# A graph-network kernel: the table that steers TensorE in its building stage packed eight steps to a word, and VectorE's key comparisons made for two steps at once

## The chip, the cores and the metric

The kernel runs as one program on one core of a Trainium2 chip. The metric is the time on the device, in microseconds, of one execution; less is better. A profiled execution gives a span (first to last instruction) and the rows quoted here. TensorE's clock has two levels, 1.2 and 2.4 GHz; a row gives the granted clock of a stretch as a share of the higher one.

## What is computed

Four graph layers on 6250 nodes of 64 features and 206250 edges, sorted by destination, each with one of four types:

```python
h = relu(layernorm(x));  x = x + attention(h, edges)          # softmax over a node's edges
h = relu(layernorm(x));  x = x + graph_conv(h, src, dst)      # degree-normalised sum
h = relu(layernorm(x));  x = x + message_mlp(h, edge_attr, src, dst)
h = relu(layernorm(x));  x = x + gru_4_steps(h, src, dst, edge_type)
# a step of the last one:
transformed = einsum('nd,khd->knh', feat, W) + b[:, None, :]
a = segment_sum(transformed[edge_type, src], dst)
feat = gru_cell(a, feat)
```

Three of the four layers need sums over a node's edges. The kernel gets them as dense products with an adjacency table: for a pair of neighbouring destination nodes, a block of 128 rows by 392 columns that counts, for each source node (128 places within a block of sources) and each combination of block of sources, type and which of the two destinations (392), the edges there are.

## The kernel before, in words

The stages are: tables from the edge list (to 329 us of the span), **building** of the adjacency table (329 to 3154 us), attention and graph convolution, the edge MLP, and the four steps of the last layer. The change touches the building stage and the tables made for it.

Edges come in tiles of 128. A pair of destinations may lie across tiles, so the work is a list of `BSTEPS` = 4859 steps; a step adds one tile's edges to one pair's block. There are 3248 pairs (`VW`), so two blocks out of about three steps are finished.

- **VectorE** (`hots_of`, L1802 to L1808) makes for each step two arrays of zeros and ones in a ring of 16 slots, `hots`: three comparisons (TENSOR_SCALAR) of a row of numbers in 16 bits with one 32-bit key a partition: L1805 over 128 columns with `key_lo`, L1806 over 98 with `key_u`, L1807 over 294 with `key_hi`. It waits on `step_done` for a free slot.
- **TensorE** (`count`, L1117 to L1131) runs two matmuls a step: L1127 multiplies the two parts of the slot (128 x 128 by 128 x 392) and adds into one of the 8 banks of `ps`; L1130 is a one-column product of zeros that marks the next bank as fresh and raises `step_done`. Which bank stands in a table, `steptab`, worked out on the chip: a word a step holds both column offsets (`>> 12` and `% 4096`). A second row of it holds, for each group of 4 steps (`BATCH`), the count of evictions that must have happened.
- The loop is written out for 64 steps (`SWEEP`) and runs 75.9 sweeps. `words` (L1109 to L1115) loads 16 words of the table into registers of TensorE's sequencer with one TENSOR_LOAD (all at L1112): once a sweep the 16 waits, which stand four words apart, and at steps 0, 16, 32 and 48 the words of 16 steps, which stand side by side. That is five loads a sweep.
- Before each group of 4 the sequencer waits for `hot_made` (L1125, L1126) and `evicted`. Before each matmul it does register arithmetic that turns the word into an address; the profile calls it FUSED_REGOPS.
- **ScalarE** (`evict`, L831 to L844) copies each finished block from its bank to `stagebuf`, with a table of its own (L835). **SyncE** (`keep`, from L616) stores 16 finished blocks at a time to HBM, 203 such events of two transfers each. **GpSimd** (`mark`) tells ScalarE when a part of `stagebuf` is free.

```python
nc.tensor.matmul(ps[:, bass.ds(held["banks"][j % STEPW] >> 12, 2 * COMBS)], hots[:, j % BRING, 0:P], ...)      # L1127
nc.tensor.matmul(ps[:, bass.ds(held["banks"][j % STEPW] % 4096, 1)], zero16[:, :], zero16[:, 0:1], ...)          # L1130
nc.vector.tensor_scalar(hots[:, j, 0:P], count_lo[:, :], part(key_lo[:, :], k, 1), None, ALU.is_equal)           # L1805
```

Ahead of the stage VectorE works out the table's columns (L1685 to L1694), TensorE turns them, L1700 copies them to `tabi`, and SyncE sends them through HBM into `steptab`. Right before the first step L1796 to L1800 derive `key_u` from `key_hi`: one copy, and three times a TENSOR_SCALAR and a TENSOR_TENSOR over 4864 columns in 32 bits. VectorE, TensorE, ScalarE, SyncE and GpSimd each run a program of their own in the order written; semaphores alone tie them.

Of the kernel before, what the change touches and what calls it, by code (L numbers as in the profile page):

```python
# [7 lines left out]
P = 128  # L8
# [3 lines left out]
NB = -(-N // P)  # L12
# [68 lines left out]
STEPW, VIRTW, BATCH = 16, 16, 4  # L81
ENDBITS = 13
SWEEP = 64
PRE = 8
# [69 lines left out]
def build(nc, a, out):  # L154
    ctx = ExitStack()
    with ctx:
# [16 lines left out]
        step_rows = dram("step_rows", (3 * BC, P), I32)  # L173
# [9 lines left out]
        key_u = early[:, 0:BPAD]  # L183
# [56 lines left out]
        tabcols = here("tabcols", [P, 3 * BC])  # L240
        tabi = here("tabi", [P, P], I32)
# [316 lines left out]
        def _(sp):  # L558
# [41 lines left out]
            def table(n, rows, count, into, first=0):  # L600
# [3 lines left out]
                sp.wait_ge(tab_stored, 16 * (n + 1))  # L604
# [4 lines left out]
            table(0, step_rows, 3, steptab)  # L609
# [4 lines left out]
            sp.wait_ge(tab_loaded, 16 * 10)  # L614
# [16 lines left out]
            sp.wait_ge(hot_made, BSTEPS)  # L631
# [85 lines left out]
        def _(pool):  # L717
# [58 lines left out]
            pool.wait_ge(tab_loaded, 16 * 10)  # L776
# [243 lines left out]
        def _(pe):  # L1020
# [53 lines left out]
            turn_table(0, 3 * BC)  # L1074
# [31 lines left out]
            pe.wait_ge(tab_loaded, 16 * 10)  # L1106
# [1152 lines left out]
```

## Time and profile before

| | |
|---|---|
| median of 3 runs | 14162.31 us (14157.45 to 14164.72) |
| the profiled execution's own time | 14159.53 us |
| its span | 14157.8 us |
| building stage, first TensorE instruction of the loop to the last matmul | 329.8 to 3153.4 us |
| busy in the whole span | TensorE 10878.2 us (77%), VectorE 6203.7 (44%), ScalarE 3496.2 (25%), GpSimd 4392.1 (31%) |
| granted clock, whole span | 0.895 |

An instruction's duration in a row runs from its start to its end; instructions of one engine overlap, so what one costs in a stream is the distance between starts. Rows of a sequencer carry a q (PEldq, DVEq, ACTq): loads of registers, register arithmetic, branches. A sequencer handles them one after the other, and an engine's instruction isn't sent before those ahead of it are done. "Idle before it" names what ended last before an instruction by the profile's own inference.

### The profile page before, as it was taken

What the parts mean: (1) busy time and instruction counts of PE and PEld (TensorE: products, weight loads), DVE (VectorE), ACT (ScalarE), POOL (GpSimd) and SP (SyncE); (2) the same over time, 40 slices, a digit from 0 to 9 for tenths busy, and PEclk for the clock granted to TensorE, in tenths of its full rate; (3) what the DMA queues carried; (4) which work ended last, traced back from release to release, by engine and by line L of the source; (5) the groups of instructions that cost most, each with busy time, mean ns of one, the idle gap of its engine ahead of it and who ended that gap; (6) DMA issues with size and microseconds to landing.
All of it is one profiled execution on the core that took longest, in us unless ns stands there. A gap on an engine that the chain in (4) does not pass through costs nothing.

```text
span 14157.8 us, 274727 instructions
## 1 busy us (share of the span) xinstructions
PE 10878.2 (77%) x60251; PEld 6423.2 (45%) x60252; DVE 6203.7 (44%) x28648; ACT 3496.2 (25%) x9549; POOL 4392.1 (31%) x3429
## 2 busy tenths in 40 slices
PE   2666656559997677777777777777789999999999
PEld 2333333333334555555555555555644444444443
DVE  6999999885662433333333343334221111111111
ACT  0555545553330222222222222222100000000000
POOL 2000000000000688888888888888200000000000
PEclk8676676769998899999999999999689999999999
DMA  2333333332226233333333333333579899899898
GB/s 93 114 115 115 115 113 114 111 128 87 94 89 264 37 42 42 42 42 42 42 42 42 42 42 42 42 42 42 46 288 348 330 355 350 336 353 348 336 348 308
DMA packets 1120461, 2096.68 MB, mean 148 GB/s; under 512 B 372941, under 2 KB 982880, under 8 KB 1012496
## 3 DMA queue, kind: packets, MB, share of 16 engines
q1 hardware_dynamic: 823736, 1913.57, 37.9%
q0 software_dynamic: 295904, 174.34, 12.0%
q8 instruction: 249, 4.08, 0.1%
q14 instruction: 572, 4.69, 0.1%
HBM read 1630.27 MB, written 457.23 MB: 147 GB/s over the span
## 4 chain that ended last, share of the span: by engine, by line
PE 51%; issue 20%; POOL 13%; DVE 9%; DMA 2%; ACT 1%; DVEq 1%; SPq 1%; POOLq 1%; ACTq 0%; another core or an unknown queue 0%
PE ps L1479 16%; PE ps L1484 8%; PE ps L1127 8%; POOL G L491 7%; POOL reverse L811 7%; PE ps L1182 4%; DVE hots L1807 2%; DVE hots L1805 2%; PE ps L1173 2%; DMA reverse<-SD,sidx 2%; DVE hots L1806 2%; PE ps L1331 1%; PE ps L1342 1%; PE ps L1282 1%; PE ps L1332 1%
## 5 line engine op out<-in xcount | busy, mean ns | idle before, releaser
L811 POOL DMA_INDIRECT reverse<-SD,sidx x1660 | 2649.2, 1596 | 555.5 <-issue 496.8
L1127 PE MATMUL ps<-hots 128*128 128x392 f16 x4859 | 1709.1, 440 | 1111.3 <-DVE hots L1807 564.9
L1479 PE MATMUL ps<-chunk,feat 128*128 128x512 f16 (+1 forms) x10192 | 2278.6, 375 | 15.0 <-DVE feat L2169 14.0
L491 POOL DMA_INDIRECT G<-h_table,idx x1660 | 1649.8, 994 | 1942.8 <-issue 1929.7
L2006 DVE TENSOR_TENSOR acc<-acc,ps 128x132 f32 x1660 | 485.5, 292 | 3014.4 <-PE ps L1345 2960.2
L841 ACT ACTIVATE stagebuf<-ps 128x392 f32 x3248 | 1438.2, 508 | 1416.1 <-PE ps L1130 1351.6
L1342 PE MATMUL ps<-MS,OH 128*128 128x128 f32 x3320 | 773.9, 316 | 1194.0 <-issue 798.1
L1479 PEld LDWEIGHTS ps<-chunk,feat 128*128 128x128 bf16 x10192 | 943.4, 98 | 1301.2 <-issue 308.0
L1807 DVE TENSOR_SCALAR hots<-count_hi,key_hi 128x294 f16<-128x294 f16 x4859 | 1458.6, 300 | 0.0
L918 ACT ACTIVATE SD<-ps 128x129 f32<-128x129 f32 x1660 | 462.0, 278 | 3701.8 <-DMA reverse<-SD,sidx 3692.0
L1805 DVE TENSOR_SCALAR hots<-count_lo,key_lo 128x128 f16<-128x128 f16 x4859 | 1240.3, 255 | 258.6 <-PE ps L1130 258.1
L1342 PEld LDWEIGHTS ps<-MS,OH 128*128 128x128 f32 x3320 | 545.0, 198 | 1741.4 <-issue 1717.9
L1127 PEld LDWEIGHTS ps<-hots 128*128 128x128 f16 x4859 | 593.8, 122 | 1622.2 <-issue 1351.3
L1331 PE MATMUL ps<-early,OT 128*128 128x256 f32 x3320 | 1081.3, 409 | 251.4 <-issue 225.2
L2105 DVE TENSOR_TENSOR summed<-ps,upper 64x512 f32<-64x512 f32 (+1 forms) x208 | 139.5, 671 | 2580.9 <-ACT upper L971 2580.8
L1806 DVE TENSOR_SCALAR hots<-count_hi,early 128x98 f16<-128x98 f16 x4859 | 1235.8, 254 | 0.0
L1484 PE MATMUL ps<-chunk,feat 128*64 128x512 f16 (+1 forms) x10192 | 1212.5, 377 | 0.0
L1332 PE MATMUL ps<-big,OT 128*128 x3320 | 1047.3, 399 | 0.0
L1130 PE MATMUL ps<-zero 128*128 128x1 bf16 x4859 | 950.8, 196 | 0.0
L798 POOL DMA_INDIRECT slot_rows<-first_table,slot_of x2 | 1.9, 956 | 2914.2 <-DMA first_table<-H 2913.9
L1345 PE MATMUL ps<-MS,EQ 128*128 128x129 f32 x3320 | 813.4, 328 | 0.0
L1484 PEld LDWEIGHTS ps<-chunk,feat 128*64 128x64 bf16 x10192 | 515.0, 109 | 655.8 <-issue 301.3
(417 smaller groups left out, 14411.3 us busy)
## 6 DMA issues: line engine op xcount, KB each, us to landing
chunk<-adj SPq DMA_DIRECT2D x720, 1792.0 KB, 9.0
adj<-stagebuf SPq DMA_DIRECT2D x406, 784.0 KB, 5.6
chunkA<-adj SPq DMA_DIRECT2D x48, 1792.0 KB, 6.7
chunk<-adj SPq DMA_DIRECT2D x60, 1232.0 KB, 6.8
G<-in_edge SPq DMA_DIRECT2D x1660, 32.0 KB
G<-h_table,idx POOLq DMA_INDIRECT x1660
reverse<-SD,sidx POOLq DMA_INDIRECT x1660
reverse<-acc SPq DMA_DIRECT2D x4, 3225.0 KB, 20.0
```

Of the source, the lines that this page charges most:

```text
L491: nc.gpsimd.indirect_dma_start(G[:, j, 0:width], None, table, bass.IndirectOffsetOnAxis(idx[:, j:j + 1], 0))\
L811: nc.gpsimd.indirect_dma_start(reverse[j % R], bass.IndirectOffsetOnAxis(sidx[:, j:j + 1], 0), SD[:, j % R, :], None, compute_op=ALU.add). ...
L841: nc.scalar.activation(stagebuf[:, bass.ds(held["word"][j] >> ENDBITS, SLEN)].rearrange("p (x c) -> p x c", c=BLK)[:, :, 0:2], bank[j % 8] ...
L1127: nc.tensor.matmul(ps[:, bass.ds(held["banks"][j % STEPW] >> 12, 2 * COMBS)], hots[:, j % BRING, 0:P], hots[:, j % BRING, P:P + 2 * COMBS] ...
L1331: nc.tensor.matmul(bank[2 + j % 2][:, 0:2 * M], OT[:, j % 2, 0:P], w("edge"), start=True, stop=False)
L1332: nc.tensor.matmul(bank[2 + j % 2][:, 0:2 * M], OT[:, j % 2, P:2 * P], big[:, bass.ds(b * 2 * M, 2 * M)], start=False, stop=True).then_inc ...
L1342: nc.tensor.matmul(bank[6][:, 0:M], OH[:, j % HOT, :], MS[:, j % MR, 0:M], start=True, stop=True)
L1479: nc.tensor.matmul(bank[k % 2][:, 0:cols], feat[0][:, hi, 0:2, :].rearrange("p a d -> p (a d)"), columns(chunk4, i % DRING, m, cols), star ...
L1484: last = nc.tensor.matmul(bank[k % 2][half:half + D, 0:cols], feat[0][:, hi, 2, :], columns(chunk4, i % DRING, m, cols), start=False, stop ...
L1805: nc.vector.tensor_scalar(hots[:, j, 0:P], count_lo[:, :], part(key_lo[:, :], k, 1), None, ALU.is_equal)
L1806: nc.vector.tensor_scalar(hots[:, j, P:P + 2 * NB], count_hi[:, 0:2 * NB], part(key_u, k, 1), None, ALU.is_equal)
L1807: nc.vector.tensor_scalar(hots[:, j, P + 2 * NB:P + 2 * COMBS], count_hi[:, 2 * NB:2 * COMBS], part(key_hi[:, :], k, 1), None, ALU.is_equa ...
```

## The change

Three things change in the building stage.

1. **TensorE's table.** A step's bank is kept as 3 bits, eight steps to a word; two group waits of 12 bits share a word. So 8 words of banks and 8 of waits serve 64 steps, and they stand side by side in one row: one load of 16 words a sweep in place of five of 16. Addresses are now worked out as `word >> 3 * i`, `% 8 * 512` for L1139 (before L1127) and `+ 1, % 8 * 512` for L1142 (before L1130), with multiply and add for size and base in both as before. Every second group takes one shift more for its wait.
2. **VectorE's comparisons.** `hots` is a ring of 8 slots for two steps each, the two interleaved: element i of step 0, element i of step 1. A slot is made by three TENSOR_TENSOR instructions of 16-bit operands: the row of numbers (each twice) against the two keys of the pair, read again for every column. Keys are kept in 16 bits. TensorE reads its operands from `hots` at every second element.
3. **The tables' making.** The packing is done by VectorE in 12 small instructions where L1700 was one copy; five small ones ahead of it go. Two transfers and one load replace one and three on SyncE's queue. `key_u` is derived in 16 bits.

```diff
-STEPW, VIRTW, BATCH = 16, 16, 4
+HG = 2
+HGROUPS = -(-BSTEPS // HG)
+HRING = BRING // HG
+VIRTW, BATCH = 16, 4
+PACK = 8
...
+SWEEPW = 2 * SWEEP // PACK
+SWEEPS = P // SWEEP
+BROW = 64
...
-        key_u = early[:, 0:BPAD]
+        key_u = early[:, 0:BPAD // 2].bitcast(F16)
...
-        key_lo = here("key_lo", [P, BPAD])
-        key_hi = here("key_hi", [P, BPAD])
-        steptab = here("steptab", [P, BPAD], I32)
+        key_lo = here("key_lo", [P, BPAD], F16)
+        key_hi = here("key_hi", [P, BPAD], F16)
+        steptab = here("steptab", [1, BC * SWEEPS * SWEEPW], I32)
...
-        count_lo = here("count_lo", [P, P], F16)
-        count_hi = here("count_hi", [P, 2 * COMBS], F16)
+        count_lo = here("count_lo", [P, P, HG], F16)
+        count_hi = here("count_hi", [P, 2 * COMBS, HG], F16)
...
-        hots = here("hots", [P, BRING, P + 2 * COMBS], F16)
+        hots = here("hots", [P, HRING, P + 2 * COMBS, HG], F16)
...
-        hots_f = stagebuf[:, 0:2 * BPAD].bitcast(F32)
+        hots_f = stagebuf[:, 0:BPAD]
...
-            table(0, step_rows, 3, steptab)
+            sp.wait_ge(tab_copied, 1)
+            for kind, row in enumerate((BROW, 0)):
+                sp.dma_start(step_rows[:, :, kind, :], tabi[row:row + BC, 0:P // PACK].rearrange("c (s w) -> c s w", s=SWEEPS))\
+                    .then_inc(tab_stored, 16)
+            sp.wait_ge(tab_stored, 32)
+            sp.dma_start(steptab[0:1, :], step_rows.rearrange("(o c) s k w -> o (c s k w)", o=1)).then_inc(tab_loaded, 16)
...
-            def words(row, k, n, stride, top):
+            def words(it):
                 _, v = nc.values_load_multi_w_load_instructions(
-                    steptab[row:row + 1, k:k + (n - 1) * stride + 1:stride] if known(k) else
-                    steptab[row:row + 1, bass.ds(k, n, step=stride)], engines=(pe.engine,),
-                    min_val=0 if row else 1, max_val=top,
+                    steptab[0:1, it * SWEEPW:(it + 1) * SWEEPW] if known(it) else steptab[0:1, bass.ds(it * SWEEPW, SWEEPW)],
+                    engines=(pe.engine,), min_val=0, max_val=max(8 ** PACK - 1, (VW + 8) * 4097),
                     skip_runtime_bounds_check_because="the path's tables are made of counts within these bounds")
                 return v
 
             def count(k, j, it):
                 if j == 0:
-                    held["free"] = words(0, k + BATCH - 1, SWEEP // BATCH, BATCH, VW + 8)
-                if j % STEPW == 0:
-                    held["banks"] = words(32, k, STEPW, 1, 7 * 512 * 4097)
+                    held["words"] = words(it)
                 if j % BATCH == 0:
-                    pe.wait_ge(hot_made, min(k + BATCH, BSTEPS) if known(k) else k + BATCH)
-                    pe.wait_ge(evicted, held["free"][j // BATCH] & 4095)
-                nc.tensor.matmul(ps[:, bass.ds(held["banks"][j % STEPW] >> 12, 2 * COMBS)], hots[:, j % BRING, 0:P],
-                                 hots[:, j % BRING, P:P + 2 * COMBS],
+                    free, odd = held["words"][SWEEPW // 2 + j // PACK], j // BATCH % 2
+                    pe.wait_ge(hot_made, min((k + BATCH) // HG, HGROUPS) if known(k) else it * (SWEEP // HG) + (j + BATCH) // HG)
+                    pe.wait_ge(evicted, (free >> 12) & 4095 if odd else free & 4095)
+                window = held["words"][j // PACK] >> 3 * (j % PACK)
+                nc.tensor.matmul(ps[:, bass.ds(window % 8 * 512, 2 * COMBS)], hots[:, j // HG % HRING, 0:P, j % HG],
+                                 hots[:, j // HG % HRING, P:P + 2 * COMBS, j % HG],
                                  start=False, stop=True, skip_group_check=True)
-                nc.tensor.matmul(ps[:, bass.ds(held["banks"][j % STEPW] % 4096, 1)], zero16[:, :], zero16[:, 0:1],
+                nc.tensor.matmul(ps[:, bass.ds((window + 1) % 8 * 512, 1)], zero16[:, :], zero16[:, 0:1],
                                  start=True, stop=True, skip_group_check=True).then_inc(step_done, 1)
...
-            link(scalar_(i1, i0, 7, 9, ALU.bitwise_and, ALU.arith_shift_left))
-            link(copy_(f7, i1))
-            link(scalar_(f0, step_w, 1.0, None, ALU.add))
-            link(copy_(i0, f0))
-            link(scalar_(i1, i0, 7, 9, ALU.bitwise_and, ALU.arith_shift_left))
-            link(nc.vector.memset(tabcols[:, 2 * BC:3 * BC], 0.0))
-            link(copy_(tabcols[:, BC:2 * BC], i1))
-            both_(out=tabcols[:, BC:2 * BC], in0=f7, scalar=4096.0, in1=tabcols[:, BC:2 * BC], op0=ALU.mult,
-                  op1=ALU.add).then_inc(tab_cols, 1)
+            link(scalar_(i1, i0, 7, None, ALU.bitwise_and))
+            copy_(tabcols[:, BROW:BROW + BC], i1).then_inc(tab_cols, 1)
...
-            copy_(tabi[0:3 * BC, :], bank[7][0:3 * BC, 0:P]).then_inc(tab_copied, 1)
+            turned_free, turned_bank = (bank[7][row:row + BC, 0:P].rearrange("c (w i) -> c w i", i=PACK) for row in (0, BROW))
+            pack_free, pack_bank = packed[0:BC, :], packed[BROW:BROW + BC, :]
+            link(copy_(pack_free, turned_free[:, :, BATCH - 1]))
+            link(both_(out=pack_free, in0=turned_free[:, :, PACK - 1], scalar=4096.0, in1=pack_free, op0=ALU.mult, op1=ALU.add))
+            link(copy_(pack_bank, turned_bank[:, :, 0]))
+            for i in range(1, PACK):
+                link(both_(out=pack_bank, in0=turned_bank[:, :, i], scalar=float(8 ** i), in1=pack_bank, op0=ALU.mult, op1=ALU.add))
+            link(copy_(tabi[0:BC, 0:P // PACK], pack_free))
+            copy_(tabi[BROW:BROW + BC, 0:P // PACK], pack_bank).then_inc(tab_copied, 1)
...
+            def keys_of(keys, k, columns):
+                return part(keys[:, :], k, HG).unsqueeze(1).to_broadcast([P, columns, HG])
+
             def hots_of(k, j, it):
-                if not (known(k) and k < BRING):
-                    v.wait_ge(step_done, k - BRING + 1)
-                nc.vector.tensor_scalar(hots[:, j, 0:P], count_lo[:, :], part(key_lo[:, :], k, 1), None, ALU.is_equal)
-                nc.vector.tensor_scalar(hots[:, j, P:P + 2 * NB], count_hi[:, 0:2 * NB], part(key_u, k, 1), None, ALU.is_equal)
-                nc.vector.tensor_scalar(hots[:, j, P + 2 * NB:P + 2 * COMBS], count_hi[:, 2 * NB:2 * COMBS],
-                                        part(key_hi[:, :], k, 1), None, ALU.is_equal).then_inc(hot_made, 1)
-            pipeline(v, BSTEPS, BRING, 0, lambda it, j: stage(BSTEPS, BRING, it, j, 0, hots_of))
+                if not (known(k) and k < HRING):
+                    v.wait_ge(step_done, k * HG - BRING + HG)
+                nc.vector.tensor_tensor(hots[:, j, 0:P, :], count_lo[:, :, :], keys_of(key_lo, k, P), ALU.is_equal)
+                nc.vector.tensor_tensor(hots[:, j, P:P + 2 * NB, :], count_hi[:, 0:2 * NB, :], keys_of(key_u, k, 2 * NB), ALU.is_equal)
+                nc.vector.tensor_tensor(hots[:, j, P + 2 * NB:P + 2 * COMBS, :], count_hi[:, 2 * NB:2 * COMBS, :],
+                                        keys_of(key_hi, k, 2 * COMBS - 2 * NB), ALU.is_equal).then_inc(hot_made, 1)
+            pipeline(v, HGROUPS, HRING, 0, lambda it, j: stage(HGROUPS, HRING, it, j, 0, hots_of))
```

TensorE, at the head of a sweep, before. ISA is the register arithmetic ahead of a matmul, REGISTER_ALU a single register operation:

```order
563 L134 UNCONDITIONAL_BRANCH
564 L134 ISA
565 L1112 TENSOR_LOAD steptab
566 L1112 ISA
567 L1112 TENSOR_LOAD steptab
568 L1125 REGISTER_ALU
569 L1126 REGISTER_ALU [waits hot_made]
570 L1127 ISA [waits evicted]
571 L1127 MATMUL ps<-hots 128x392
572 L1130 ISA
573 L1130 MATMUL ps<-zero 128x1
```

The same place after the change, and the head of the second group of 4:

```order
570 L1125 TENSOR_LOAD steptab
571 L1136 ISA
572 L1137 REGISTER_ALU [waits hot_made]
573 L1139 ISA [waits evicted]
574 L1139 MATMUL ps<-hots 128x392
...
589 L1136 REGISTER_ALU
590 L1137 REGISTER_ALU [waits hot_made]
591 L1137 REGISTER_ALU
592 L1139 ISA [waits evicted]
593 L1139 MATMUL ps<-hots 128x392
```

One load stands where two stood (three more go later in the sweep), and each step keeps two ISA and two MATMUL; what an ISA holds grew from three register operations to five (at a word's first step four for L1139).

VectorE in the loop, one step before:

```order
285 L1804 REGISTER_ALU
286 L1805 ISA [waits step_done]
287 L1805 TENSOR_SCALAR hots<-count_lo,key_lo 128x128
288 L1806 REGISTER_ALU
289 L1806 TENSOR_SCALAR hots<-count_hi,early 128x98
290 L1807 REGISTER_ALU
291 L1807 TENSOR_SCALAR hots<-count_hi,key_hi 128x294
```

and two steps after the change:

```order
261 L1821 ISA
262 L1822 ISA [waits step_done]
263 L1822 TENSOR_TENSOR hots<-count_lo,key_lo 128x256
264 L1823 REGISTER_ALU
265 L1823 TENSOR_TENSOR hots<-count_hi,early 128x196
266 L1824 REGISTER_ALU
267 L1824 TENSOR_TENSOR hots<-count_hi,key_hi 128x588
```

Three instructions now make two steps, twice as wide each; `early` is the memory that holds `key_u`.

## Rows read from the trace of the kernel before

**Rows 1.** Busy time by stretch, 600 us inside the building stage.
```profile
core 0: us, PE busy (x) PEld busy (x) DVE busy (x) ACT busy (x) POOL busy (x), PEclk, DMA share, GB/s
1000.00:1600.00 600.00, 365.01 (x2072) 220.52 (x2072) 543.98 (x3098) 303.49 (x684) 0.00 (x0) 0.70 0.34 113
```
**Rows 2.** Waits, 329 to 3160 us: who waited for whom, us in total, times, longest.
```profile
PEld ps L1127 <- issue: 1351.3, 1217, 9.4
PE ps L1127 <- DVE hots L1807: 564.9, 277, 5.8
DVE hots L1805 <- PE ps L1130: 258.1, 100, 5.7
```
**Rows 3.** TensorE's timeline: start us, duration us, instruction; firsts of groups of 4, and two steps.
```profile
1500.51 0.49 PE L1127 MATMUL ps<-hots 128*128 128x392 f16 x1
1500.86 0.49 PE L1127 MATMUL ps<-hots 128*128 128x392 f16 x1
...
1506.93 0.34 PE L1127 MATMUL ps<-hots 128*128 128x392 f16 x1 [1.44 <-DVE hots L1807]
...
1508.39 0.49 PE L1127 MATMUL ps<-hots 128*128 128x392 f16 x1 [0.16 <-issue]
```
**Rows 4.** Line L1112, whole trace; then two stretches of one sweep (min/median/max ns).
```profile
L1112 PEldq TENSOR_LOAD <-steptab x380: 1102/1274/7260, 329.9 to 3147.1; - x190
...
L1112 PEldq TENSOR_LOAD <-steptab x3: 1103/2002/5232, 1104.9 to 1117.4; - x3
...
L1112 PEldq TENSOR_LOAD <-steptab x2: 1107/1862/2617, 1125.5 to 1132.6; - x2
```
**Rows 5.** TensorE's timeline on both sides of a single load and of a sweep's head.
```profile
1097.06 0.34 PE L1127 MATMUL ps<-hots 128*128 128x392 f16 x1
1098.86 0.51 PE L1127 MATMUL ps<-hots 128*128 128x392 f16 x1 [1.46 <-DVE hots L1807]
...
1104.21 0.34 PE L1127 MATMUL ps<-hots 128*128 128x392 f16 x1
...
1111.80 0.50 PE L1127 MATMUL ps<-hots 128*128 128x392 f16 x1 [7.25 <-issue]
```
**Rows 6.** Register work of TensorE's sequencer by line: count, min/median/max ns.
```profile
L1127 PEldq FUSED_REGOPS  x4859: 72/76/84, 335.2 to 3153.1; - x195
L1130 PEldq FUSED_REGOPS  x4859: 73/78/89, 335.4 to 3153.3; - x195
L1112 PEldq FUSED_REGOPS  x296: 52/52/58, 368.3 to 3108.0; - x148
L1332 PEldq FUSED_REGOPS  x1660: 55/55/77, 4703.1 to 9989.1; - x185
L134 PEldq FUSED_REGOPS  x131: 44/68/78, 364.2 to 10249.0; - x131
```
**Rows 7.** VectorE's timeline, the same instruction five steps apart.
```profile
1500.44 0.25 DVE L1805 TENSOR_SCALAR hots<-count_lo,key_lo 128x128 f16<-128x128 f16 x1 [0.95 <-PE ps L1130]
...
1503.07 0.25 DVE L1805 TENSOR_SCALAR hots<-count_lo,key_lo 128x128 f16<-128x128 f16 x1
```
**Rows 8.** VectorE's groups by shape: count, busy us, mean ns.
```profile
L1643 DVE TENSOR_SCALAR cmps<-iota,cf 128x4864 bf16<-128x4864 int16 x13 | 18.3, 1482 | 1.0 <-PE ps L1041 1.0
L1800 DVE TENSOR_TENSOR early<-early,stagebuf 128x4864 f32<-128x4864 f32 x3 | 15.7, 5225 | 0.1
L1799 DVE TENSOR_SCALAR stagebuf<-early 128x4864 f32<-128x4864 f32 x3 | 8.1, 2694 | 0.1
```
**Rows 9.** VectorE's timeline: starts of two-source instructions; one small one of the tables.
```profile
5604.82 0.69 DVE L526 TENSOR_TENSOR OH<-iota,dloc 128x512 f32<-128x512 f32 x1
5605.43 0.17 DVE L1994 TENSOR_TENSOR TH<-iota,typ 128x16 f32<-128x16 f32 x1
5605.51 0.35 DVE L2022 TENSOR_SCALAR EQ<-ps,key 128x128 f32<-128x128 f32 x1
...
210.19 0.22 DVE L1689 TENSOR_SCALAR cf<-cf 128x38 f32<-128x38 f32 x1
```
**Rows 10.** ScalarE in the stage: two evictions in the timeline, its table's loads by line.
```profile
1501.50 0.94 ACT L841 ACTIVATE stagebuf<-ps 128x392 f32 x2 [0.20 <-PE ps L1130]
...
L835 ACTq TENSOR_LOAD <-path x203: 1012/1022/1222, 302.2 to 3146.1; - x102
```

More of the change, by code:

```diff
@@ L172, in build @@
         key_table = dram("key_table", (TP, 3 * P))
-        step_rows = dram("step_rows", (3 * BC, P), I32)
+        step_rows = dram("step_rows", (BC, SWEEPS, 2, SWEEPW // 2), I32)
         virt_rows = dram("virt_rows", (3 * VC, P), I32)
@@ L240, in build @@
         tabcols = here("tabcols", [P, 3 * BC])
+        packed = here("packed", [P, P // PACK])
         tabi = here("tabi", [P, P], I32)
@@ L603, in table @@
                 sp.dma_start(rows, tabi[0:rows.shape[0], :]).then_inc(tab_stored, 16)
-                sp.wait_ge(tab_stored, 16 * (n + 1))
+                sp.wait_ge(tab_stored, 16 * (n + 2))
                 lines = rows.rearrange("(q c) p -> q (c p)", q=count)
@@ L613, in _ @@
             sp.dma_start(endrow, virt_rows.rearrange("(q c) p -> q (c p)", q=3)[0:1, :]).then_inc(tab_loaded, 16)
-            sp.wait_ge(tab_loaded, 16 * 10)
+            sp.wait_ge(tab_loaded, 16 * 8)
             def keep(k, j, it):
@@ L630, in _ @@
             pipeline(sp, NEV, 6, 0, lambda it, j: stage(NEV, 6, it, j, 0, keep))
-            sp.wait_ge(hot_made, BSTEPS)
+            sp.wait_ge(hot_made, HGROUPS)
             sp.dma_start(X_, a["x"].rearrange("(b p) d -> p b d", p=P)).then_inc(x_loaded, 16)
@@ L774, in _ @@
                         .then_inc(key_gathered[h], 16)
-            pool.wait_ge(tab_loaded, 16 * 10)
+            pool.wait_ge(tab_loaded, 16 * 8)
             def words(row, k, top):
@@ L1073, in _ @@
                 last.then_inc(cmp_used, 1)
-            turn_table(0, 3 * BC)
+            turn_table(0, BROW + BC)
             pe.wait_ge(asked, 2)
@@ L1103, in _ @@
                 last.then_inc(key_turned, 1)
-            pe.wait_ge(tab_loaded, 16 * 10)
+            pe.wait_ge(tab_loaded, 16 * 8)
             pe.wait_ge(key_copied, 10)
@@ L1625, in _ @@
             link(copy_(at[:, :], at_i[:, :]))
-            link(copy_(count_lo[:, :], iota16[:, 1:P + 1]))
-            link(copy_(count_hi[:, :], iota16[:, 0:2 * COMBS]))
+            link(copy_(count_lo[:, :, :], iota16[:, 1:P + 1].unsqueeze(2).to_broadcast([P, P, HG])))
+            link(copy_(count_hi[:, :, :], iota16[:, 0:2 * COMBS].unsqueeze(2).to_broadcast([P, 2 * COMBS, HG])))
             link(nc.vector.memset(weigh[:, :, :], 1.0))
@@ L1684, in _ @@
             copy_(tidx[:, :], f0).then_inc(step_known, 1)
+            link(nc.vector.memset(tabcols[:, :], 0.0))
             link(scalar_(tabcols[:, 0:BC], step_w, 2.0, None, ALU.add))
             link(copy_(i0, step_w))
-            link(scalar_(i1, i0, 7, 9, ALU.bitwise_and, ALU.arith_shift_left))
-            link(copy_(f7, i1))
-            link(scalar_(f0, step_w, 1.0, None, ALU.add))
-            link(copy_(i0, f0))
-            link(scalar_(i1, i0, 7, 9, ALU.bitwise_and, ALU.arith_shift_left))
-            link(nc.vector.memset(tabcols[:, 2 * BC:3 * BC], 0.0))
-            link(copy_(tabcols[:, BC:2 * BC], i1))
-            both_(out=tabcols[:, BC:2 * BC], in0=f7, scalar=4096.0, in1=tabcols[:, BC:2 * BC], op0=ALU.mult,
-                  op1=ALU.add).then_inc(tab_cols, 1)
+            link(scalar_(i1, i0, 7, None, ALU.bitwise_and))
+            copy_(tabcols[:, BROW:BROW + BC], i1).then_inc(tab_cols, 1)
             for c in range(CG):
@@ L1745, in _ @@
             v.wait_ge(tab_turned, 2)
-            v.wait_ge(tab_stored, 16)
+            v.wait_ge(tab_stored, 32)
             copy_(tabi[0:3 * VC, :], bank[7][0:3 * VC, 0:P]).then_inc(tab_copied, 1)
@@ L1777, in _ @@
             v.wait_ge(tab_turned, 3)
-            v.wait_ge(tab_stored, 32)
+            v.wait_ge(tab_stored, 48)
             copy_(tabi[0:6, :], bank[7][0:6, 0:P]).then_inc(tab_copied, 1)
@@ L1786, in _ @@
                       op0=ALU.is_equal, op1=ALU.mult).then_inc(key_masked, 1)
-            v.wait_ge(tab_loaded, 16 * 10)
+            v.wait_ge(tab_loaded, 16 * 8)
             place = virttab[96:97, 0:VPAD - 1]
```

## The prediction

> **What bounds the kernel now.** I read the busy time of a stretch inside the building stage first [rows 1]: VectorE 544 of 600 us, TensorE 365, granted clock 0.70, DMA share 0.34. That looks like a stage paced by VectorE. The waits say otherwise [rows 2]: VectorE waits 258 us for TensorE's `step_done`, and the largest idle time by far, 1351 us, stands before TensorE's weight load with "issue" as its cause, which is time in which nothing but its own sequencer held it.
>
> So I price the sequencer. Without a load between them, groups of 4 steps start 1.46 us apart (1506.93 to 1508.39), although those four matmuls ran at the high clock (0.34 us each). At the low clock (0.49 us) one step follows another after 0.35 [rows 3], four of them 1.42 us, which the 1.46 also covers. The pace is thus the sequencer's at either clock. A sweep of 64 steps has 16 groups: 23.4 us. The loads come on top [rows 4]: the five of one sweep took 5.23 us at its head, then 1.10, 2.00, 1.11 and 2.62, in sum 12.06. Each costs a restart too: around the load of 1.10 us at 1097 the matmuls of neighbouring groups start 1.80 us apart, around the sweep's head 7.59 [rows 5], where a step across groups without a load takes about 0.5. That is 0.2 us beyond the load for a single one, and 0.75 beyond the two (6.34) at the head. Sum: 23.4 + 12.1 + 0.75 + 3 x 0.2 = 36.8 us. The stage lasts 3153.3 - 329.9 = 2823 us [rows 4, 6] for 75.9 sweeps, 37.2 us each. TensorE's sequencer accounts for the whole stage. VectorE needs 2.63 us for five steps [rows 7], 33.6 us a sweep, and sits in the shadow with 3.6 us to spare, 275 us in all, against 258 measured. The 565 us that the waits give to L1807 can't be a real wait of that size, since the groups leave no room for it; VectorE's signal merely comes last before a matmul that the loads had delayed.
>
> **The change, part by part.**
>
> *Loads.* Four of five go. The remaining one reads 16 words side by side. What does it cost? The cheapest was 1.10 us; the three of the sweep that stood alone took 2.00, 1.11 and 2.62, mean 1.91 [rows 4]. The sweep's first, 5.23 us, has two things apart from them: its words are four apart, and it stands at the loop's head. ScalarE's load of 16 neighbouring words stands at the head of its loop as well and takes 1.01 to 1.22 us [rows 10], so I put the difference down to the spread words and take 2.0. Bounds: 1.1 and 5.2.  With it one restart and the branch, 0.55. Loads and restarts fall from 13.4 (13.8 in the average sweep) to 2.55 us.
>
> The Trainium skill, "Runtime: NRT & Kernel Launch", section on instruction fetch, gives a TENSOR_LOAD about 200 ns a register, however many it loads. An estimate by that page is 3.2 us for the 16 words and a time of 13686. This trace has 69 ns a word where 16 neighbours took 1.10 us, and more than the page where they lie four apart (5.23 us, 327 ns), so I keep the row.
>
> *Register work.* It grows, and it is on the path. Before a matmul three operations (shift or remainder, multiply, add) take 76 and 78 ns [rows 6]. Plain multiplies and adds take 52 for three (L1112), 55 for four (L1332), and 68 where most are the five of a loop's head (L134). So a division costs 24 more than a plain operation, a remainder 26. The new ones: divide, remainder, two multiplies, add: 68 + 24 + 26 = 118, in one step of eight without the division, about 84; mean 114. Add, remainder, two multiplies, add: 68 + 26 = 94. Together 208 where 154 stood, 54 ns a step; I take 56, since the numbers divided are longer. A group: 1.46 + 4 x 0.056 + half a REGISTER_ALU (0.02) = 1.70 us, a sweep 27.2. Bounds: with 5 ns for an added plain operation and 26 for the remainder it is 40 ns a step, group 1.63; with twice the price for division and remainder some 80 to 90, group 1.82.
>
> *TensorE in sum:* 27.2 + 2.55, 29.8 us a sweep, and 0.1 because the stores fill more of each sweep: 29.9. Saved: (37.2 - 29.9) x 75.9 = 554 us.
>
> *VectorE.* No row has a two-source instruction with all operands in 16 bits. From above: in 32 bits an element costs (5225 - 160) / 4864 = 1.04 ns [rows 8]. From below: 16-bit one-source, 1482 ns for 4864 columns, 0.26 with some 0.2 us fixed. I take 0.52, because for one source the step from 32 bits (2694 ns, 0.52) to 16 bits halves an element's price, and the two-source row is the nearer one to start from. The fixed part: an instruction of 16 columns is followed after 0.08 us, one of 512 after 0.61 [rows 9], so about 0.065. A pair of steps: (256 + 196 + 588) x 0.52 + 3 x 0.065 = 0.74 us, a sweep 23.5 us in place of 33.6: still in TensorE's shadow, now by 6.4 us. Only if TensorE's sequencer were cheaper than that would this gain show.
>
> The Trainium skill, "VectorE: DVE Perf Modes", section on the TRN2 errata, speaks against this part: 58 cycles fixed for an instruction of either kind. With two elements a cycle for two sources and four for one, from its tier table, a pair would cost 0.63 us before and 0.72 after, an estimate by that page. The rows speak against that for what is removed (1.05 us for a pair), so I count the part as a gain of VectorE's own; on the path neither shows.
>
> *TensorE's array* reads every second element. I take no cost; no row has such an operand. The group's pace leaves 0.425 us for a step that takes 0.35 at the low clock.
>
> *ScalarE* has 42.8 evictions a sweep at 0.47 us or less (two in 0.94), 20 us, and 2.7 loads of 1.0 [rows 10]: under 24 us with its register work. Stores: 203 events come every 11.2 us in place of 13.9, DMA share from 0.34 to some 0.42. Both stay covered; the matmuls within a group run no denser than now.
>
> *Tables.* `key_u` in 16 bits halves its chain right before the first step: by rows 8, three of 5.23 and four of 2.69 (the copy taken like L1799) become half, 13 us saved; if the two-source ones don't speed up, 5. The packing adds 11 small linked instructions and drops five, at 0.25 us at most [rows 9]: 1.5 us. Together 11 saved, between 3 and 12. SyncE's transfers for `steptab` are issued some 60 us before they are needed.
>
> *Sum:* 14159.5 (the profiled execution's own time) - 554 - 11 = **13594.5**. The median of the runs shown lies 3 us above that execution, so I say 13597.
>
> **The rivals.**
>
> *VectorE gets no second element a cycle.* The key operand is one pair of 16-bit keys read over and over, in rows of two elements, and no row shows such an operand; the doubling may need longer runs or two plain operands. The Trainium skill, "Vector Engine (DVE) Microarchitecture Reference", section 5.1, has a two-source instruction fall to one element a cycle where an operand repeats a single element, and says that a row read again and again still runs doubled. If the doubling fails here, a pair costs 1040 x 1.04 + 0.195 = 1.28 us, a sweep 40.9, and VectorE sets the stage: 2430 x 1.28 = 3110 us from its first comparison, 287 us longer than now; with 4 us off the tables, **14443**, slower. It decides from 0.72 ns an element ((0.94 - 0.195) / 1040; 0.94 is TensorE's pace for a pair). For it: no row shows the doubling for two sources. Against: one-source instructions do double with 16 bits [rows 8].
>
> *The load stays dear.* If the loop's head and not the spread words makes the first load long, it remains 5.2 us or so: 3.3 x 75.9 = 250 less saved, **13850**. ScalarE's rows speak against it.
>
> *The array pays for the stride.* At twice the time a column a step at the low clock takes 0.68 us, a sweep 46 us: up to 14831, slower too. It decides above 0.425 us a step. Nothing in the rows speaks for it.
>
> *The gain is eaten elsewhere* (evictions, stores): within 30 us of the time before. The idle times of ScalarE speak against it.
>
> **How the numbers follow.** My case has a chance of 0.76 and its own range, with a group of 1.63 to 1.82 us and a load of 1.1 to 3 us, not both at their ends, is 13500 to 13740. Dear load 0.07, VectorE at one element 0.11, stride 0.03, eaten 0.03. The range of 13490 to 13870 holds the first two. Faster by over 0.2% (about what a measurement of this kernel can tell from no change): 0.84; within 0.02; slower 0.14.
>
> **What would show it.** Right: one TENSOR_LOAD a sweep of 1.1 to 3.9 us; FUSED_REGOPS at L1139 near 115 ns and L1142 near 95; groups 1.70 us apart at either clock; VectorE's three starts 0.74 us apart for a pair and its idle time for `step_done` grown to some 480 us; the stage about 2270 us. Wrong: VectorE without idle time and TensorE's groups waiting for `hot_made`; L1139's matmul longer than 0.51 us; evictions that hold TensorE up.

## The result and the profile after

The changed kernel takes 13660.12 us (median; 13654.69 to 13663.5) where the kernel before took 14159.88 beside it: a ratio of 0.9647, 95% interval 0.963 to 0.9664. The prediction was 13597, range 13490 to 13870: right in direction, with the measured time 63 us above the forecast.

| | before | after |
|---|---|---|
| span of the profiled execution | 14157.8 us | 13653.0 us |
| first load of the table to the start of the last 392-column matmul | 329.9 to 3153.4 us | 315.4 to 2652.4 us |
| a sweep of 64 steps (that stretch by 75.9) | 37.2 us | 30.8 us |
| granted clock, whole span | 0.895 | 0.892 |

The tables ahead of the stage are 14.5 us shorter, the stage 486 us, and all that follows 4 us. So the whole gain is where the change was made. The busy time of the same stretch as [rows 1]:

```profile
core 0: us, PE busy (x) PEld busy (x) DVE busy (x) ACT busy (x) POOL busy (x), PEclk, DMA share, GB/s
1000.00:1600.00 600.00, 494.89 (x2509) 255.02 (x2508) 502.12 (x1882) 375.64 (x828) 0.00 (x0) 0.66 0.42 139
```

More matmuls in the same time (2509 against 2072), VectorE less busy though it does more steps, stores up as forecast (DMA share 0.42). The register work and the loads of TensorE's sequencer, one line each of the rows of a source line, answer [rows 4, 6] (count: min/median/max ns, first and last start):

```profile
L1125 PEldq TENSOR_LOAD <-steptab x76: 1102/1333/3677, 315.4 to 2619.7; - x76
...
L1139 PEldq FUSED_REGOPS  x4859: 100/130/146, 316.8 to 2652.2; - x195
...
L1142 PEldq FUSED_REGOPS  x4859: 88/90/123, 317.0 to 2652.4; - x195
...
L1137 PEldq ALU_OP  x1822: 32/36/42, 316.7 to 2651.4; - x183
...
L1136 PEldq ALU_OP  x1110: 36/36/36, 346.9 to 2617.6; - x185
```

There are 76 loads where there were 380. Their mean is 1.92 us. The register work before a pair of matmuls has a mean of 126 + 91.5 = 217.5 ns, against 75.5 + 77.3 = 153 before. TensorE's timeline has the firsts of groups of four 1.88 and 1.66 us apart (every second group has one more register instruction for its wait):

```profile
1500.86 0.34 PE L1139 MATMUL ps<-hots 128*128 128x392 f16 x1 [0.20 <-ACT stagebuf L854]
...
1502.74 0.34 PE L1139 MATMUL ps<-hots 128*128 128x392 f16 x1 [0.36 <-ACT stagebuf L854]
...
1504.40 0.34 PE L1139 MATMUL ps<-hots 128*128 128x392 f16 x1 [0.20 <-issue]
```

Over the whole stage, from the first L1139 matmul of one group to that of the next, a group without a load takes 1.777 us on average and one with the sweep's load 4.14. Fifteen of the first and one of the second are 30.8 us, the measured sweep. (Six groups near the stage's end take over 3 us, because TensorE waits there for ScalarE's evictions; without them the average is 1.770.) The clock does not set this pace: groups whose matmuls all ran at the low clock take 1.774 us on average, those at the high one 1.767 (before: 1.467 and 1.466). VectorE's timeline answers [rows 7]; two slots start 0.76 us apart:

```profile
1500.07 0.29 DVE L1822 TENSOR_TENSOR hots<-count_lo,key_lo 128x256 f16<-128x256 f16 x1
1500.28 0.25 DVE L1823 TENSOR_TENSOR hots<-count_hi,early 128x196 f16<-128x196 f16 x1
1500.45 0.46 DVE L1824 TENSOR_TENSOR hots<-count_hi,key_hi 128x588 f16<-128x588 f16 x1
1500.83 0.28 DVE L1822 TENSOR_TENSOR hots<-count_lo,key_lo 128x256 f16<-128x256 f16 x1
```

The waits, for [rows 2] (us in total, times, longest):

```profile
PEld ps L1139 <- issue: 607.5, 1221, 4.5
DVE hots L1822 <- PE ps L1142: 338.5, 653, 4.4
PE ps L1139 <- issue: 212.9, 516, 4.4
PE ps L1139 <- DVE hots L1824: 102.8, 160, 1.9
...
PE ps L1139 <- ACT stagebuf L854: 59.0, 163, 2.0
```

Idle time put down to the sequencer has halved and is still the largest. VectorE still waits for TensorE.

### The profile page after: what moved, and what is told of

It reads as the page before. It is cut to its first block, busy times and chain, and to the rows that moved or that the text cites. A ratio compares the mean times of both kernels' runs of the same rounds, so it can differ in the third digit from the quotient of the medians.

```text
span 13653.0 us, 258090 instructions
## 1 busy us (share of the span) xinstructions
PE 11057.9 (81%) x60251; PEld 6361.4 (47%) x60252; DVE 5587.9 (41%) x21367; ACT 3529.7 (26%) x9549; POOL 4391.0 (32%) x3429
## 4 chain that ended last, share of the span: by engine, by line
PE 54%; issue 19%; POOL 16%; DVE 4%; DMA 2%; ACT 1%; POOLq 1%; SPq 1%; DVEq 0%; ACTq 0%; another core or an unknown queue 0%
PE ps L1491 16%; PE ps L1139 11%; PE ps L1496 9%; POOL G L499 8%; POOL reverse L824 8%; PE ps L1194 4%; PE ps L1185 2%; DMA reverse<-SD,sidx 2%; DVE hots L1824 1%; PE ps L1294 1%; PE ps L1343 1%; PE ps L1354 1%; PE ps L1344 1%; POOLq L823 1%; PE ps L1357 1%
## 5 line engine op out<-in xcount | busy, mean ns | idle before, releaser
L1139 PE MATMUL ps<-hots 128*128 128x392 f16 x4859 | 1893.7, 449 | 428.4 <-issue 212.9
L854 ACT ACTIVATE stagebuf<-ps 128x392 f32 x3248 | 1470.5, 506 | 884.5 <-PE ps L1142 804.8
L1824 DVE TENSOR_TENSOR hots<-count_hi,key_hi 128x588 f16<-128x588 f16 x2430 | 1112.5, 458 | 0.0
L1139 PEld LDWEIGHTS ps<-hots 128*128 128x128 f16 x4859 | 494.0, 102 | 987.4 <-issue 607.5
L1142 PE MATMUL ps<-zero 128*128 128x1 bf16 x4859 | 936.0, 193 | 0.0
L1822 DVE TENSOR_TENSOR hots<-count_lo,key_lo 128x256 f16<-128x256 f16 x2430 | 706.2, 291 | 387.4 <-PE ps L1142 338.5
L984 ACT ACTIVATE upper<-ps 64x512 f32<-64x512 f32 (+1 forms) x208 | 121.4, 584 | 2760.5 <-PE ps L1496 2760.4
```

What stands on the lines that cost most here:

```text
L854: nc.scalar.activation(stagebuf[:, bass.ds(held["word"][j] >> ENDBITS, SLEN)].rearrange("p (x c) -> p x c", c=BLK)[:, :, 0:2], bank[j % 8] ...
L1139: nc.tensor.matmul(ps[:, bass.ds(window % 8 * 512, 2 * COMBS)], hots[:, j // HG % HRING, 0:P, j % HG], hots[:, j // HG % HRING, P:P + 2 * ...
L1142: nc.tensor.matmul(ps[:, bass.ds((window + 1) % 8 * 512, 1)], zero16[:, :], zero16[:, 0:1], start=True, stop=True, skip_group_check=True). ...
L1824: nc.vector.tensor_tensor(hots[:, j, P + 2 * NB:P + 2 * COMBS, :], count_hi[:, 2 * NB:2 * COMBS, :], keys_of(key_hi, k, 2 * COMBS - 2 * NB ...
```

## The experiments

**Theory one** is the prediction's: TensorE's sequencer (loads of the table, register work) sets the pace of the stage. **Theory two**: VectorE, busy 544 of 600 us before [rows 1], is the bound, and its shorter comparisons are the gain. Each ratio is against runs of the kernel before on the same chip. Those took 14142 us beside both halves, the four loads and the sweeps of 128 and 14156 or 14149 beside the others, so two medians of this table can differ by up to 18 us through the chip alone; where such a difference matters I use the stage's length.

| run | median us | ratio to before (95%) | stage, first 392-column matmul to the end of the last, us |
|---|---|---|---|
| before | 14159.88 | 1 | 2818.5 |
| the change | 13660.12 | 0.9647 (0.963 to 0.9664) | 2335.9 |
| VectorE's part alone | 14128.86 | 0.9992 (0.9982 to 1.0002) | 2816.9 |
| table's part alone | 13878.87 | 0.9812 (0.9795 to 0.983) | 2555.7 |
| keys in 32 bits | 14470.19 | 1.0222 (1.0202 to 1.0242) | 3132.3 |
| four loads a sweep | 14097.87 | 0.9969 (0.9957 to 0.9982) | 2783.5 |
| before, loads swapped | 14150.74 | one run, no interval | 2813.2 |
| and for remainder | 14885.79 | 1.0516 (1.0495 to 1.0537) | 3561.7 |
| two steps to a word | 13679.55 | 0.9662 (0.9646 to 0.9678) | 2356.3 |
| sweeps of 128 | 13607.36 | 0.9622 (0.9605 to 0.9639) | 2289.6 |
| one key wait in eight steps | 13614.75 | 0.9621 (0.9605 to 0.9637) | 2291.6 |
| both of these | 13571.61 | 0.959 (0.9574 to 0.9606) | 2247.7 |

### Each half of the change alone

The kernel before with what the diff does to `hots`, the keys and `hots_of`:

```diff
-                nc.vector.tensor_scalar(hots[:, j, 0:P], count_lo[:, :], part(key_lo[:, :], k, 1), None, ALU.is_equal)
+                nc.vector.tensor_tensor(hots[:, j, 0:P, :], count_lo[:, :, :], keys_of(key_lo, k, P), ALU.is_equal)
...
```

> The kernel before with VectorE's part of the change alone (keys in 16 bits, two steps per comparison), the building table and TensorE's loads as before. Theory one, TensorE's sequencer sets the pace of the building stage (23.4 us of issue, 12.1 us of loads and some 1.5 us of restarts a sweep): VectorE's work falls from 33.6 to about 24.3 us a sweep and its wait for step_done grows by as much, the stage stays at about 2820 us and the kernel at 14,150 us (ratio 0.998 to 1.001). Theory two, VectorE (busy 544 of 600 us before) is what bounds the stage: most of the 500 us gained is here, the kernel comes to some 13,700 us, ratio about 0.968.

Measured: 0.9992, not to be told from no change, and the stage 1.6 us shorter. TensorE reads every second element of `hots` here too, so this run also shows that the stride costs the stage nothing. Its waits (L1130 and L1133 are the two matmuls in this kernel, L1811 and L1813 the first and last comparison):

```profile
PEld ps L1130 <- issue: 1350.6, 1230, 9.4
...
DVE hots L1811 <- PE ps L1133: 956.3, 304, 8.9
...
PE ps L1130 <- DVE hots L1813: 156.1, 111, 5.5
```

Its busy time by stretch, columns as above:

```profile
1000.00:1600.00 600.00, 365.38 (x2066) 218.90 (x2064) 394.20 (x1551) 304.86 (x686) 0.00 (x0) 0.70 0.35 115
```

VectorE's busy time in the stretch fell from 544 to 394 us, and all of that became waiting. Its wait grew from 258 to 956 us, by 698, or 9.2 us a sweep: what its comparisons lost (33.6 - 24.3). The 565 us that the waits of before gave to VectorE's signal [rows 2] fell to 156 with nothing gained. They were no real wait. Theory two is out for the kernel before.

The other half is the changed kernel with VectorE as before (and its keys in 32 bits):

> The changed kernel with VectorE's comparisons as before (one step at a time, 32-bit keys), the packed table and the one load a sweep kept. Theory one: TensorE's sequencer would need 30.8 us a sweep, but VectorE needs 64 times 0.525 us, 33.6 us, so the pace becomes VectorE's: stage near 2560 us, kernel near 13,880 us, ratio 0.980 (0.977 to 0.984). Theory two, VectorE is the bound in both kernels: about 14,150 us, ratio 0.999. If TensorE's side alone were the whole gain, as the prediction has it where it says that VectorE's saving does not show, 13,660 us, ratio 0.965.

Measured: 0.9812, the stage 2555.7 us for the 2560 expected. VectorE is now busy without a gap in the busy time by stretch:

```profile
1000.00:1600.00 600.00, 464.50 (x2288) 236.45 (x2288) 600.00 (x3431) 343.84 (x754) 0.00 (x0) 0.55 0.38 126
```

And TensorE waits for it (waits of the same kernel):

```profile
PE ps L1139 <- DVE hots L1821: 306.3, 375, 4.4
```

So one half gives 266 us (14160 x 0.0188), the other 11 with the tables, and both together 500. The 220 us or so that are missing from the sum belong to neither alone: the packed table takes TensorE below VectorE's 33.6 us a sweep, and only then is VectorE's saving worth anything.

### The rival: keys in 32 bits

```diff
-        key_lo = here("key_lo", [P, BPAD], F16)
-        key_hi = here("key_hi", [P, BPAD], F16)
+        key_lo = here("key_lo", [P, BPAD])
+        key_hi = here("key_hi", [P, BPAD])
```

`key_u` too, all else as changed.

> The changed kernel with its keys in 32 bits, all else as changed: the mixed types should take VectorE's comparison from two elements a cycle to one. The pair then takes about 1.28 us (three comparisons of 0.33 to 0.63 us, 1040 elements over 0.96 GHz and the fixed part) in place of 0.76, so VectorE sets the pace: 2430 pairs times 0.52 us more, against some 2.4 us a sweep that it had spare: kernel near 14,440 us (the prediction's rival). If the rate of two elements does not hang on the keys' width: 13,660 us.

Measured: 14470, slower than before. VectorE's busy time in the stretch is 600 of 600 us, and its timeline has a slot in 1.29 us:

```profile
1499.75 0.41 DVE L1822 TENSOR_TENSOR hots<-count_lo,key_lo 128x256 f16<-128x256 f16 x1
1500.09 0.34 DVE L1823 TENSOR_TENSOR hots<-count_hi,early 128x196 f16<-128x196 f16 x1
1500.36 0.75 DVE L1824 TENSOR_TENSOR hots<-count_hi,key_hi 128x588 f16<-128x588 f16 x1
1501.04 0.41 DVE L1822 TENSOR_TENSOR hots<-count_lo,key_lo 128x256 f16<-128x256 f16 x1
```

The distance to the next start is 0.27 us for 196 elements and 0.68 for 588: 1.05 ns an element. With the 16-bit keys it is 0.17 and 0.38, or 0.54 ns. The rival's price (14443) was right: a pair at one element takes 1.29 us and VectorE then sets the stage. What it gave as the reason was not, since the changed kernel repeats its pair of keys just as this one does and is not slowed by it. The width of the keys decides.

### What a load costs

```diff
-                if j == 0:
+                if j % 16 == 0:
                     held["words"] = words(it)
```

> The changed kernel with the same 16 words loaded again at every 16th step, four loads a sweep in place of one. Theory one: three further loads a sweep of about 1.9 us each with about 0.2 us of emptied pipe, 6.3 us a sweep over 76 sweeps: +480 us, kernel near 14,140 us. If loads that follow soon on one another find the queue free of stores (the second load of the kernel before took 1.1 us each time), 3 times 1.2 to 1.9 us: 13,950 to 14,140 us. Theory two, VectorE or ScalarE bounds the changed stage: under +150 us.

Measured: 438 us more than the change, for 3 x 76 = 228 further loads 1.92 us each; the mean of all its loads is 1.95. The stage is 447.6 us longer (2783.5 for 2335.9), and the durations of the loads in sum grew by as much, from 145.7 to 593.3 us. So the loads stand on the path in full, and the 0.2 us for an emptied pipe that I had added to each (480 us in all) do not show. Then the question which of the two oddities made the first load of the kernel before dear:

```diff
-                if j == 0:
-                    held["free"] = words(0, k + BATCH - 1, SWEEP // BATCH, BATCH, VW + 8)
                 if j % STEPW == 0:
                     held["banks"] = words(32, k, STEPW, 1, 7 * 512 * 4097)
+                if j == 0:
+                    held["free"] = words(0, k + BATCH - 1, SWEEP // BATCH, BATCH, VW + 8)
```

> The kernel before with the two loads at the head of a sweep in the other order: sixteen neighbouring bank words first, then the sixteen words that lie four apart. Before, the spread load came first and took 3.8 to 7.3 us (mean 5.4), the neighbouring one behind it always 1.10. If the spread words are what is dear: neighbouring load now 1.1 to 3.9 us (mean 2.0, like the third to fifth), spread load behind it about 4 us each time; sum 6.0, no change of the kernel. If the place at the head of the sweep is what is dear: neighbouring load 4 to 7 us and the spread one behind it 1.1 us.

Measured: the spread words are dear. The rows of the load's line at the head of one sweep, first the load at 1103.3 alone, then with the one behind it (2437 and 3799 ns):

```profile
L1112 PEldq TENSOR_LOAD <-steptab x1: 2437/2437/2437, 1103.3 to 1103.3; - x1
...
L1112 PEldq TENSOR_LOAD <-steptab x2: 2437/3118/3799, 1103.3 to 1105.9; - x2
```

Over 76 sweeps the neighbouring words, now first, take 1.10 to 3.85 us, mean 2.02, and the spread ones behind them 3.80 to 7.18, mean 4.45. The cheapest load is 69 ns a word side by side and 237 ns a word four apart.

### What register work costs

```diff
-                nc.tensor.matmul(ps[:, bass.ds(window % 8 * 512, 2 * COMBS)], hots[:, j // HG % HRING, 0:P, j % HG],
+                nc.tensor.matmul(ps[:, bass.ds((window & 7) * 512, 2 * COMBS)], hots[:, j // HG % HRING, 0:P, j % HG],
...
-                nc.tensor.matmul(ps[:, bass.ds((window + 1) % 8 * 512, 1)], zero16[:, :], zero16[:, 0:1],
+                nc.tensor.matmul(ps[:, bass.ds((window + 1 & 7) * 512, 1)], zero16[:, :], zero16[:, 0:1],
```

> The changed kernel with the remainder by eight written as a bitwise and. The compiler doesn't fuse the and, nor the shift and the addition ahead of it: per step four register instructions of 36 ns stand beside two shorter fused ones of some 50 to 60 ns, about 250 ns in place of 217.5. Theory one, the sequencer sets the pace: 33 ns times 4859 steps, 160 us more, 13,820 us (13,740 to 13,900 for fused ones of 45 to 75 ns). Theory two, VectorE or ScalarE sets it: no change, 13,660 us. If remainders are what is dear in the fused ones, faster than 13,660 us.

Measured: 1226 us more, where 160 were expected. Direction right, price wrong by a factor of eight. The rows of the two lines:

```profile
L1142 PEldq ALU_OP  x9718: 36/36/36, 316.4 to 3877.7; - x199
L1142 PEldq FUSED_REGOPS  x4859: 46/46/51, 316.6 to 3877.8; - x195
...
L1139 PEldq ALU_OP  x9110: 32/36/41, 316.2 to 3877.4; - x199
L1139 PEldq FUSED_REGOPS  x4859: 46/46/51, 316.3 to 3877.5; - x195
```

The fused instructions did shrink, to 46 ns each: 125.5 ns a step less, 610 us in all. Yet the stage is 1226 us longer, so the 18828 separate instructions cost 1836 us, 97.5 ns each and not their 36. In the trace's records one of them begins 97 ns after the other: 36 of its own and 61 in which the queue does nothing. A step inside a group is now 0.66 us, and the timeline has "issue" before matmuls inside a group too:

```profile
1502.31 0.51 PE L1139 MATMUL ps<-hots 128*128 128x392 f16 x1 [0.22 <-issue]
1502.97 0.51 PE L1139 MATMUL ps<-hots 128*128 128x392 f16 x1 [0.16 <-issue]
```

This shows who sets the pace: VectorE, ScalarE and the stores do the same work as in the changed kernel.

### Trading words for operations

Bank offsets times 512, two to a word (`word % 3585`, `word // 3585`), so that no division and remainder meet in one address:

```diff
-                window = held["words"][j // PACK] >> 3 * (j % PACK)
-                nc.tensor.matmul(ps[:, bass.ds(window % 8 * 512, 2 * COMBS)], hots[:, j // HG % HRING, 0:P, j % HG],
+                word = held["words"][j // BPACK]
+                window = word // 3585 if j % BPACK else word % 3585
+                nc.tensor.matmul(ps[:, bass.ds(window, 2 * COMBS)], hots[:, j // HG % HRING, 0:P, j % HG],
...
-                nc.tensor.matmul(ps[:, bass.ds((window + 1) % 8 * 512, 1)], zero16[:, :], zero16[:, 0:1],
+                nc.tensor.matmul(ps[:, bass.ds((window + 512) % 4096, 1)], zero16[:, :], zero16[:, 0:1],
```

> The changed kernel with the bank words packed two steps to a word, each field already times 512 (32 words a sweep and 8 with the waits' counts, read by two loads at the head of the sweep), so that each address is one operation shorter in the division or remainder and has no multiplication by 512. Theory one, the sequencer's register work and loads set the pace: per step the work before the first matmul falls from 126 ns to about the 76 of the kernel before, that before the second from 91.5 to some 80 to 90, 3.3 to 3.9 us a sweep less; the loads grow from 1.9 us to 3.2 (32 words, as in the sweep of 128) and 0.6 to 1.1: 1.9 to 2.4 us more. Net 0.9 to 2.0 us over 76 sweeps: 13,510 to 13,590 us, ratio to before 0.954 to 0.960. Theory two, another engine bounds the changed stage: 13,660 us or above.

A miss: 13680, no gain. The rows of its two lines of register work (here L1142 stands before the large matmul, L1145 before the small one) say why:

```profile
L1142 PEldq FUSED_REGOPS  x4859: 77/82/100, 320.4 to 2676.3; - x195
...
L1145 PEldq FUSED_REGOPS  x4859: 96/101/104, 320.6 to 2676.5; - x195
```

The first fell to 83 ns on average, but the second rose from 91.5 to 102, though it has a multiplication less: it seems that the remainder by 4096 of a number up to 4096 costs more than that by 8 of one up to 8, for nothing else in this address grew. So 32 ns a step were saved and not 51 to 61, 156 us in the stage. The loads went from 146 to 309 us in sum (32 words 3.36 us on average, 8 words 0.71), 163 more. That sums to 7 us more; the stage is 20 us longer (2356.3 for 2335.9), and the other 13 are not explained.

### Fewer loads, fewer instructions

`SWEEP = 128`, nothing else:

> The changed kernel with sweeps of 128 steps and one load of 32 words: half as many loads and restarts of the loop, twice the unrolled program. Theory one: of two loads of 1.92 us and two restarts of 0.57 us, one load of some 2.2 to 3.3 us and one restart are left: 1.1 to 2.2 us in 128 steps, over 38 such sweeps 42 to 84 us less than the changed kernel, so 13,575 to 13,620 us, ratio to before 0.959 to 0.962. Theory two, VectorE's or ScalarE's work bounds the changed stage: no change from 13,660 us. If the longer program has to be fetched while it runs, slower than 13,660 us.

Measured: 13607 us, the stage 46 us shorter, inside the forecast. The one load of 32 words has a mean of 3.24 us, where two of 16 took 3.83 (row of the load's line):

```profile
L1125 PEldq TENSOR_LOAD <-steptab x38: 2127/2978/5445, 313.8 to 2538.4; - x38
```

Next the price of 97 ns put to use:

```diff
-                    pe.wait_ge(hot_made, min((k + BATCH) // HG, HGROUPS) if known(k) else it * (SWEEP // HG) + (j + BATCH) // HG)
+                    if not odd:
+                        pe.wait_ge(hot_made, min((k + PACK) // HG, HGROUPS) if known(k) else it * (SWEEP // HG) + (j + PACK) // HG)
```

> The changed kernel, but TensorE waits for VectorE's keys once in eight steps and not in four: seven or eight register additions a sweep fewer and as many waits. What the run with the bitwise and showed, that each separate register instruction of TensorE's queue takes 36 ns and some 61 ns pass until the next begins: 8 times 97 ns, 0.78 us a sweep, 59 us over 76 sweeps: 13,600 us, ratio to before 0.961 (0.958 to 0.965). If only the 36 ns count: 22 us, 13,638 us. If VectorE, which now must be eight steps ahead, becomes the wait (it has some 5 us a sweep to spare): slower than 13,660 us.

Measured: 13615 us, the stage 44 us shorter. The separate additions fell by 592 (from 1110), by the row of their line:

```profile
L1137 PEldq ALU_OP  x518: 36/36/36, 348.9 to 2572.1; - x173
```

That is 75 ns each, with the waits that went along: well over 36, somewhat under 97. And both together:

> The changed kernel with both edits that took instructions from TensorE's queue: sweeps of 128 steps (53 us in the run before) and one wait for VectorE's keys in eight steps (59 us by the price of 97 ns an instruction). Theory one, the queue of TensorE sets the pace and the two add up: 13,550 us, ratio to before 0.957 (0.955 to 0.960). If VectorE or ScalarE is reached on the way: 13,570 to 13,610 us.

Measured: 13571.6 us, ratio 0.959. The number alone doesn't decide, as it lies in the range of theory one and also at the lower end of the other one's 13,570 to 13,610. The stage does: it is 88 us shorter than the change's (46 + 44 = 90), so the two add up. The forecast of 13,550 was low because it took 53 and 59 us for the parts. This version beats both kernels; its interval lies clear of the change's. VectorE's wait for TensorE is down from 338 to 180 us, so VectorE still isn't reached:

```profile
DVE hots L1823 <- PE ps L1143: 180.0, 137, 6.4
```

## Why the prediction was right, and where not

*What bounds the kernel before: right.* The stage was TensorE's sequencer's, against what [rows 1] suggest at first. The half with VectorE alone shows it.

*Loads: right.* Taken 2.0 us, measured 1.92; with the restart 2.55 taken and 4.14 - 1.78 = 2.36 measured. The choice of the spread words as the cause was right too. The rule of the Trainium skill, "Runtime: NRT & Kernel Launch", of about 200 ns a register would have given 3.2 us. It is stated there for registers loaded from HBM, while `steptab` lies in SBUF, and this trace does not bear it out: 69 ns a word at the least and 120 on average. That its estimate of the time, 13686, lies nearer to the result than mine is chance, since the missing time was in the register work.

*Register work: direction right, size too small.* This is the step that failed, as "a group: 1.46 + 4 x 0.056 + half a REGISTER_ALU (0.02) = 1.70 us". Measured: 1.777. Of the missing 0.077 us, 0.034 is the fused work, which grew by 64.6 ns a step and not 56 (217.4 for 152.8). The error lies at L1139 (126 for 114), while L1142 was 91.5 for 94. I had taken 68 ns as the price of the plain operations from the loop's head; two multiplications and an addition cost 46, and a remainder then costs from at least 32 ns (78 - 46, [rows 6]) to some 56 (102 - 46), it seems by the numbers that it gets. Another 0.029 is the separate instruction: half of one a group is 49 ns and not the 20 taken. The six groups that waited for ScalarE are 0.007, and as much is left over. In a sweep that is 16 x 0.077 = 1.23 us too little, against 0.19 too much for the load and 0.1 for the stores: 0.94 us, or 71 us in the stage, where the miss was 68 (486 for 554), and 63 in all.

*VectorE: price right, its worth told wrongly.* The pair took 0.76 us for 0.74. But the text said "Only if TensorE's sequencer were cheaper than that would this gain show", and "on the path neither shows". That does not follow from its own numbers: VectorE needed 33.6 us a sweep and TensorE was to need 29.9. Without the shorter comparisons the stage would have stopped at 33.6. The run with the table alone shows this part to be worth 220 us. The total stood only because both parts were in it. Its wait was forecast at some 480 us and measured at 338, though by the starts of its slots it stood still for 488. The trace accounts for the difference: idle time is counted from the end of L1824, which lies 0.08 us behind the point where the next slot can start (0.46 against 0.38 us), and 1276 slots started late, which makes 102 us; 387 us of idle time stand before L1822 in all, 338 of them put down to TensorE.

The Trainium skill, "VectorE: DVE Perf Modes", section on the TRN2 errata, spoke against this part with 0.63 us for a pair before and 0.72 after. Its 0.72 is near the 0.76 measured. The 0.63 isn't borne out: the rows had 1.05 us. In the trace of the kernel before, the comparisons of 98, 128 and 294 columns are followed by the next after 156, 162 and 206 ns (medians): 0.255 ns a column and 0.13 us fixed for each, twice what the same difference leaves for TENSOR_TENSOR here (0.17 - 196 x 0.54 ns = 0.065).

*The array and the stride: right.* L1139's matmul takes 339 to 508 ns, where L1127's took 326 to 508. *Evictions and stores: right in the main.* Of TensorE's 59 us of waits for ScalarE, nine of 1.4 to 2.0 us make up 15, and the kernel before had about as much. *Tables:* 14.5 us saved, 11 taken.

*The rivals.* One element a cycle had its price right (14470 for 14443) and its cause wrong: not the repeated pair of keys but the keys' width decides. The dear load fell with the swapped loads.

## What to carry to other kernels

When two engines run close to one another, price what the second would need alone before calling its saving worthless: a cut on the first engine is worth only the distance to the second. A share of busy time names no bound; here 544 us of 600 were in the shadow of an engine busy 365, and "issue" in the waits told it. On a queue that works out its addresses, count the instructions before their durations: here a fused chain of five operations took 130 ns, two separate instructions 2 x 97.

## What the runs showed that was not expected

- A separate register instruction on TensorE's queue costs about 97 ns, 36 of them shown as its duration (1836 us for 18828 of them). Taking 592 out gave 75 ns each.
- A bitwise and isn't fused into the address arithmetic, a remainder is: 1226 us for one operator changed in two addresses.
- A fused instruction of two multiplications and an addition takes 46 ns; a remainder in it adds some 32 to 56 ns, it seems by its operands.
- Words of a table four apart cost 237 ns each to load into registers, side by side 69 ns, at their cheapest and at either place at the head of the sweep. Above that a load of 16 side by side takes up to 3.9 us; what stretches it was not tried.
- The pace of TensorE's steps did not depend on its granted clock: groups of four took 1.774 us at the low and 1.767 at the high level of the clock.
